# Ternary tiles of the layer part kept in two-byte values and turned by SyncE's transposing SBUF-to-SBUF transfers instead of by TensorE

## The reference, cut to what matters

```python
x = L0_attn_x                                    # (2, 1024, 512)
x = _layernorm(x + attention(x, w_in, w_out, rms_w), axis=-1)

def _L0_ffn_ref(x, weight, rram_variation):      # TH_X, SC_X = 0.33, 0.5 ; TH_W, SC_W = 0.2, 0.6
    x_q = ternary_quantize(x, TH_X, SC_X)        # 0.5, 0 or -0.5
    w_q = ternary_quantize(weight, TH_W, SC_W)
    return jnp.einsum('bsd,od->bso', x_q, w_q + rram_variation)

x = _layernorm(x + _L0_ffn_ref(x, L0_ffn_weight, L0_ffn_rram_variation), axis=-1)
```

## Time and profile before

| what | value |
|---|---|
| median of the runs | 1428.39 us (1426.57, 1430.21) |
| span of the profiled execution | 1429.2 us |
| the profiled execution's own time | not given beside its span; the span lies between the two runs |
| mean granted TensorE clock | 0.983 |
| PE busy | 1355.2 us (95%) |
| DVE, ACT, POOL busy | 1140.2 us (80%), 1087.5 us (76%), 875.7 us (61%) |
| layer part | from about 1340 us to the end |

### The profile page before, as it was taken

The page is one execution under the profiler, slowest core; times in us unless marked ns, Lnnn a source line. Parts: engine busy times, 40 slices in busy tenths (PEclk is TensorE's granted clock), DMA queues, the critical chain, the costliest instruction groups (busy, mean ns, idle before and its releaser), DMA issues.

```text
span 1429.2 us, 25089 instructions
## 1 busy us (share of the span) xinstructions
PE 1355.2 (95%) x7296; PEld 1115.2 (78%) x7296; DVE 1140.2 (80%) x3015; ACT 1087.5 (76%) x2293; POOL 875.7 (61%) x862
## 2 busy tenths in 40 slices
PE   4889999999999999999999999999999999996896
PEld 3678787888888888888888888888888888884674
DVE  4677787888797888888797888878797887965896
ACT  4668778778787878778787878778787878775674
POOL 1447557376656766376656766376646766469766
PEclk9799999999999999999999999999999999998899
DMA  6002111211101111111101111111101111011112
GB/s 206 19 20 60 42 31 31 48 35 45 35 23 49 55 29 31 46 38 45 35 24 49 53 30 31 44 40 45 34 24 49 51 32 31 25 50 41 26 46 84
DMA packets 45161, 61.79 MB, mean 43 GB/s; under 512 B 10464, under 2 KB 27104, under 8 KB 45024
## 3 DMA queue, kind: packets, MB, share of 16 engines
q1 hardware_dynamic: 45024, 60.20, 14.6%
HBM read 34.74 MB, written 4.46 MB: 27 GB/s over the span
## 4 chain that ended last, share of the span: by engine, by line
PE 75%; DVE 7%; ACT 6%; POOL 4%; issue 4%; DMA 3%; SPq 1%; POOLq 0%; DVEq 0%; ACTq 0%
PE s L1075 17%; PE x L1087 17%; PE t L1121 14%; PE x L1105 9%; PE ot L1046 8%; PE ot L1044 8%; DMA spread<-recip_rows 2%; DVE prob L943 2%; ACT prob_hi L751 2%; ACT prob L782 2%; DVE prob_lo L1011 1%; PE x L1095 1%; PE x L1031 1%; DVE win_lo L961 1%; DVE stats L844 1%
## 5 line engine op out<-in xcount | busy, mean ns | idle before, releaser
L751 ACT ACTIVATE prob_hi<-t 128x512 fp32r<-128x512 f32 x576 | 340.2, 593 | 158.9 <-PE t L1121 152.8
L1011 DVE TENSOR_TENSOR prob_lo<-t,prob_hi 128x512 fp32r<-128x512 f32 x576 | 394.5, 686 | 64.0 <-ACT prob_hi L751 59.1
L1075 PE MATMUL s<-k_t,q_t 128*128 128x512 f32 (+3 forms) x1536 | 411.7, 373 | 28.3 <-POOL q_t L701 9.7
L782 ACT ACTIVATE prob<-prob,neg_max 128x896 f32<-128x896 f32 (+7 forms) x512 | 393.2, 769 | 31.0 <-DVE neg_max L943 29.4
L943 DVE CUSTOM_DVE_ANT_0 prob<-s,mask 128x512 f32<-128x512 f32 (+3 forms) x512 | 293.0, 586 | 74.8 <-PE s L1075 45.4
L1121 PE MATMUL t<-ident,prob 128*128 128x128 f32 x2304 | 348.2, 274 | 3.3 <-ACT prob L782 3.1
L1121 PEld LDWEIGHTS t<-ident,prob 128*128 128x128 f32 x2304 | 288.6, 141 | 78.7 <-ACT prob L782 6.3
L1075 PEld LDWEIGHTS s<-k_t,q_t 128*128 128x128 f32 x1536 | 246.4, 192 | 63.7 <-DVE neg_max L943 11.6
L724 POOL TENSOR_TENSOR o_lo<-o_raw,o_hi 128x256 fp32r<-128x256 f32 x128 | 94.8, 740 | 246.6 <-ACT o_hi L837 246.3
L1044 PE MATMUL ot<-prob_hi,v_sb 128*128 128x512 f32 x576 | 239.5, 416 | 2.3 <-DVE o_raw L993 1.5
L1046 PE MATMUL ot<-prob_lo,v_sb 128*128 128x512 f32 x576 | 232.6, 404 | 5.9 <-DVE prob_lo L1011 5.8
(11 more groups left out here) (87 smaller groups left out, 2013.2 us busy)
## 6 DMA issues: line engine op xcount, KB each, us to landing
swapped<-flat SPq DMA_DIRECT2D x320, 64.0 KB, 2.0
spread<-recip_rows SPq DMA_DIRECT2D x128, 128.0 KB
recip_rows<-turned SPq DMA_DIRECT2D x512, 0.5 KB
raw<-L_attn_w_in SPq DMA_DIRECT2D x8, 768.0 KB, 7.7
raw<-L_attn_w_out SPq DMA_DIRECT2D x8, 512.0 KB, 3.6
out<-acc SPq DMA_DIRECT2D x16, 256.0 KB, 2.0
acc<-L_attn_x SPq DMA_DIRECT2D x3, 1024.0 KB, 10.4
acc<-L_attn_x SPq DMA_DIRECT2D x4, 256.0 KB, 3.7
```

The costliest lines, as they stand in the source:

```text
L751: act.activation(prob_hi[:, u % 2, :], t_ps[u % 2][:, :], ACT.Copy).then_inc(prob_hi_done, 1)
L782: act.activation(row, row, ACT.Exp, bias=neg_max[:, kk % 4, h:h + 1], scale=-1.0, accum_out=total[:, kk % 4, h:h + 1]).then_inc(ex_done, 1)
L1011: dve.tensor_tensor(prob_lo[:, u % 2, :], t_ps[u % 2][:, :], prob_hi[:, u % 2, :].bitcast(F32), ALU.subtract).then_inc(prob_lo_done, 1)
L1075: mm = pe.matmul(s_ps[:, off:off + cols], q_t[:, h, s * P:(s + 1) * P], k_t[:, part, keys:keys + cols], start=(part == 0), stop=(part == 1))
```

## The change

The ternary tile is written in two bytes per value (bfloat16, which holds -1, 0 and 1) into the first half of its slot of `raw`. SP turns it by one transposing transfer (`dma_start_transpose`) into the second half of the same slot. ScalarE copies from there to `xq`, with the cast to the matmul's type, and TensorE has no transposes of the layer part. ScalarE's copy moves from the event `tern` to the event `ffn`. `ffn` is put at least 10 steps behind `tern`, `res` at least 6 behind `ffn`, and `out` at least 20 behind `res`; the plan of the last pass gets 20 slots behind its units instead of 15. `tern` no longer takes a bank of the ring.

```diff
-X_KINDS = ("pj", "vt", "op", "norm", "tern", "ffn")
+X_KINDS = ("pj", "vt", "op", "norm", "ffn")
+TURN_STEPS = 10
...
-    plan = Plan(BODY + (15 if last else 0), BODY)
+    plan = Plan(BODY + (20 if last else 0), BODY)
...
         for t in range(2 * NT):
-            for kind, at in zip(("ln", "x1", "tn", "tern", "ffn", "res", "out"), at_pass["LAYER"][t]):
+            ln, x1, tn, tern, ffn, res, stored = at_pass["LAYER"][t]
+            ffn = max(ffn, tern + TURN_STEPS)
+            res = max(res, ffn + 6)
+            for kind, at in zip(("ln", "x1", "tn", "tern", "ffn", "res", "out"),
+                                (ln, x1, tn, tern, ffn, res, max(stored, res + 20))):
                 put(at, (kind, t))
...
+        tern_turned = [sem(f"tern_turned{n}") for n in range(3)]
...
         def tern_tile(t):
-            return raw[:, t % 3, :]
+            return raw[:, t % 3, 0:D // 2].bitcast(BF16)
+
+        def turned_tile(t):
+            return raw[:, t % 3, D // 2:D].bitcast(BF16).rearrange("p (k q) -> p k q", k=KC)
...
+                        elif e[0] == "tern":
+                            t = e[1]
+                            sp.wait_ge(tern_done, t + 1)
+                            sp.dma_start_transpose(turned_tile(t), tern_tile(t)).then_inc(tern_turned[t % 3], 16)
...
-            def move_ternary(t, bank):
+            def move_ternary(t):
                 if t >= 2:
                     act.wait_ge(x2_done, t - 1)
-                act.activation(xq_tile(t), bank[:, :].rearrange("p (k q) -> p k q", k=KC), ACT.Copy
-                               ).then_inc(xq_done, 1)
+                act.wait_ge(tern_turned[t % 3], 16 * (t // 3 + 1))
+                act.activation(xq_tile(t), turned_tile(t), ACT.Copy).then_inc(xq_done, 1)
...
-                        if e[0] == "tern":
-                            move_ternary(e[1], wait_x_full(act, plan, g, e))
+                        if e[0] == "ffn":
+                            move_ternary(e[1])
...
-            def turn_ternary(t, bank):
-                pe.wait_ge(tern_done, t + 1)
-                for c in range(KC):
-                    mm = pe.transpose(bank[:, c * P:(c + 1) * P], tern_tile(t)[:, c * P:(c + 1) * P], ident[:, :])
-                return mm
...
-                        if e[0] == "tern":
-                            turn_ternary(e[1], bank).then_inc(x_full, 1)
-                        elif e[0] == "ffn":
+                        if e[0] == "ffn":
```

More of the change, by code:

```diff
@@ L454, in wait_x_free @@
                 eng.wait_ge(y_lo_done, what[0] + 1)
-            elif kind == "tern":
-                eng.wait_ge(xq_done, what[0] + 1)
             elif kind == "ffn":
```

## The result

The kernel after the change takes 1468.12 us, the median of two runs (1465.79 and 1470.45), against 1428.39: a ratio of 1.0275, 95% interval 1.0223 to 1.0326. It is slower by 39.7 us, where the forecast was 26. The number lies inside the predicted range of 1439 to 1474, but outside the forecast's own range of 1448 to 1460, and on the far side of the 2% line: that side had 0.40, the other 0.59. The profiled execution is the slower of the two, so what its parts add up to comes to 2.3 us more than the median.

A forecast was written before the change was run, and what follows sets the result against it. It took TensorE as the bound over most of the span, with VectorE also full from 1340 to 1400 us and a chain of waits after. 1429.2 + 14.2 + 7.9 + 3, less 0.3, gave 1454 us, range 1439 to 1474.

The forecast's parts named there:

- the forecast: Whole kernel: 1454 us, 1.8% slower, with its own range 1448 to 1460; chance 0.45.
- Instructions: Layer part: copy taken as 0.60 us, ternary and `below` kept at their four-byte medians, 0.686 and 1.50 us.
- The stalls of the body: 1340 to 1400 us: PE waits for the late copy, 18.7 us over tiles 0 to 7; body ends 14.2 us later.
- The clock: Body and tail: matmuls at half clock after PE idles, 1.6 to 1.8 us more per eight; 3 us added, bounds 0 to 14.
- The tail: From 1400 us: the transfer's latency in the chain of odd tiles adds 7.9 us, bounds -1.3 to +21.5.
- L: Time from the ternary's end to the transfer's landing, SP's issue included: taken as 4.3 us, range 2.0 to 7.7.
- 4 L - 9.3: Tail's change in us: four transfer latencies up to tile 15's matmuls, set against the time before; breaks even at 2.3 us.
- two tiles cost L + 5.2 where they cost 6.6: Tail, odd tiles: each two-tile period is one transfer latency plus 5.2 us, instead of 6.6; three such periods.
- The long transfer: Rival: transfer latency of 6.7 us makes the tail 17.5 us longer, 1466 us in all; chance 0.27.
- The short transfer: Rival: latency of 2.4 us, tail +0.3 us, the body's stalls remain, 1445 us in all; chance 0.14.
- No stalls: Rival: ScalarE level with PE at the body's copies, body -3.2 us, tail +7.9, 1435 us in all; chance 0.10.
- the other side: Rival, faster or equal: copies in time and transfer under 2.3 us, 1424.7 us in all; chance 0.04.

The follow-up runs named there:

- e1: Kernel before, TensorE still turning the tiles, with only ScalarE's copy moved from `tern` to `ffn`: 1450.59 us, ratio 1.0156.
- e2: Kernel after, with ScalarE's copy at an event of its own, some slots before `ffn`: 1447.41 us, ratio 1.0132.
- e3: Kernel after, with eight filler matmuls ahead of the wait of each `ffn` so that PE doesn't idle: 1458.05 us, ratio 1.0206.
- e4: Kernel after, with `ffn` and `res` back at their steps of before, `out` still 20 behind: 1459.13 us, ratio 1.0209.
- e11: Kernel after, with each transposing transfer issued a second time once the first has landed: 1477.26 us, ratio 1.0351.

## Why the prediction was right in direction and short in size

**Instructions.** Right: copy 0.62 for 0.60, ternary 0.690 for 0.686, `below` 1.502 for 1.50.

**The stalls of the body.** Right in mechanism, and close in size. The idle time of PE ahead of `ffn` for tiles 0 to 7 was predicted as 1.5, 2.0, 3.6, 3.1, 2.7, 2.7, 1.4, 1.7 (18.7); it is 3.5, 1.9, 3.6, 3.2, 3.0, 2.6, 2.9, 1.9 (22.7). "Matmuls wait for the copy" is 22.6 us, not some 15. e1 and e2 show that it is the copy's place: alone it costs the body 12.9 us, and undone it gives the body back to within 2.9. With the clock held up, e3's body is 15.5 us over before, beside the forecast of 14.2. In the body of the kernel after the copy waits for a transfer only once, 1.5 us.

**The clock.** This is the term that was mis-sized. It stood at 3 us with bounds 0 and 14. The bursts alone got 5.9 us longer in the body and 3.7 in the tail, and holding the clock up gave 10.1 back. I had put the stalls of 2.7 to 3.6 us at the size at which the clock had fallen, and then priced fewer than two bursts of the sixteen. In the kernel after, the body's six gaps of 2.6 us and more were followed by a burst at half clock, wholly or but for its last matmul, at tiles 0, 2, 4 and 6, by one at it in part at tile 3, and by one at full clock at tile 5 (2.62 us). Tile 0's burst was at half clock in the kernel before too, behind a gap of 0.78 us. Tile 7's, behind 1.90 us, was at it in part. So the size of the gap alone doesn't tell. At 1.7 us for a burst, the 10.1 us are the price of six, not of two.

**The postponed places.** They were taken as neutral and cost 9 us (e4), in part through the clock.

**The tail.** Two errors that hid each other. L was 2.5, not 4.3; with that, the formula 4 L - 9.3 gives +0.7, not +7.9. Measured is +12.4. With L right the whole sum would have been 1447 us, 21 short. That the forecast came as near as 14, and the time within the range, owes that much to luck.

The step that failed is "two tiles cost L + 5.2 where they cost 6.6". Tile 9 to tile 15 took 31.6 us, where three times 7.7 make 23.1. Period by period it took 8.3, 13.8 and 9.6. The first is near 7.7, and the 0.6 over it are tile 9's burst, in part at half clock. The 6.6 was read from tiles 14 and 15 alone; in the kernel before, tile 11 to 13 takes 10.0, because of ScalarE's wait for POOL's `shift`, which the prediction never mentions. And the copy's place, walked slot by slot for the body, wasn't walked in the tail: tile 12's copy went behind that wait. e1 shows what this costs without any transfer, 6.5 us in the middle period. In the kernel after, that period is 3.7 us over before, which the copy's place is more than enough to explain. The outer two are over by 1.7 and 3.0 us, which e1 doesn't have; they come with the transfer, and e11 lengthens them by 3.6 and 3.4. Why the last one is 1.9 us over L + 5.2 wasn't separated.

The other 4.0 us come ahead of tile 9 (7.0 instead of 3.0 us). Of these 2.2 are there in e1 too. Tile 9's transfer landed late besides, 4.8 us behind its issue:

```profile
1421.01 1.24 SPq L593 DMA_TRANSPOSE raw<-raw  x1
...
1422.34 0.53 SPq L570 DMA_DIRECT2D spread<-recip_rows  x1
...
1423.01 4.28 SPq L593 DMA_TRANSPOSE raw<-raw  x2
...
1427.91 0.63 ACT L748 ACTIVATE yt_hi<-raw 128x512 fp32r<-128x512 bf16 x1 [2.67 <-DMA raw<-raw]
```

**The rivals.** The long transfer gave the nearest number (1466) for a reason that is false, L of 6.7. The short transfer had L right (2.4) and the time wrong by 23 us (1445), since its sum had the same constant. "No stalls" and the other side fell with the waits of the body. The premise of the first, that ScalarE has 3 to 6 us idle in each 20, was misread besides: by the earlier trace rows it is 6.5, 3.0 and 9.6.

**What would beat both.** None of these kernels beats the one before. The nearest, four tiles by transfer, is 0.2% slower. TensorE's turn is short, and in no variant did the 0.35 to 0.44 us that it takes of PE show as a gain. A transfer with tile 12's copy kept ahead of `x1` of tile 14, and nothing else moved, wasn't tried.

## What to carry to other kernels

When work moves to another engine, ask first where the consumer's copy then stands in its engine's order: here its place alone cost 22 us of the 40, and it was a side effect of the edit. Walk the orders through the whole stretch, not only where the stall is expected: in the tail the same move put one tile's copy behind an instruction that waits for a third engine. A period is read from every pair of tiles and not from the last one (6.6, but 10.0 in the middle), and the longest wait of a view is explained first. And where an engine is full, gaps can cost twice, as gaps and as matmuls at half clock behind them.

## What the runs showed of the hardware

- A transposing SBUF-to-SBUF transfer of 128x512 two-byte values lands 2.4 to 2.5 us behind its issue where no broadcast is issued near it (104 of 108 transfers in the eleven kernels that have them; the other four took 3.3 to 3.9). The issue holds SP for 1.2 us, where stores and broadcasts hold it for 0.3 to 0.5.
- It is made of small pieces. The page counts 53865 packets, 19168 of them under 512 B; before, it was 45161 and 10464. That is 8704 / 16 = 544 small packets for each tile.
- Some land late: 5.6, 5.9, 4.6, 3.5 and 4.8 us for tiles 4, 6, 7, 8 and 9 of the kernel after. All 28 that were issued 0.6 to 1.1 us behind the broadcast `spread<-recip_rows`, in eleven kernels, took 4.6 to 6.0 us. Of the 28 with that broadcast issued 1.3 to 1.5 us after them, 18 took 2.4 to 2.5 and ten 3.5 to 5.9. It isn't a matter of transposing: in all 13 kernels where a store was issued 0.6 to 0.7 us behind that broadcast, it took 4.8 to 5.7 us instead of about 2.0, in the kernel before 5.1 (1368.41). No run took the broadcast away, so its part isn't shown by an experiment.
- A TensorE that has idled can be slow afterwards: behind 2.98 us of idle time ahead of tile 4 the granted clock was 0.50, and the matmuls started 0.42 us apart instead of 0.23; behind 2.62 us ahead of tile 5 it was 1.00. Adding 128 matmuls to the kernel after made it 10 us faster.
